# Moving gathers and low-part subtractions between GpSimd and VectorE in a three-layer interaction network

## The reference

```
prev = x
for k in 0, 1, 2:
    z = outer product of x and prev over the fields, for each example b and each of the 16 columns e
    t = z @ w[k] + bias[k]
    t = t / sqrt(sum of t*t over the units and the 16 columns)
    prev = t
features = concatenation of the three t, summed over e
```

## Time and profile before

| what | value |
|---|---|
| median of three runs | 1063.23 us (1059.57 to 1064.48) |
| the profiled execution's own time | 1061.89 us |
| its span, first to last instruction | 1060.2 us |
| PE busy | 1027.2 us, 97% |
| DVE busy | 974.6 us, 92% |
| POOL busy | 872.0 us, 82% |
| ACT busy | 795.4 us, 75% |

### The profile page before, as it was taken

One profiled execution on the slowest core, in us unless ns is written; L12 is line 12 of the kernel. 1 busy time (PEld: TensorE's weight loads), 2 busy tenths in 40 slices (PEclk: granted clock), 3 DMA queues, 4 the chain that ended last, 5 costly groups with the idle time before them and its releaser, 6 DMA issues.

```text
span 1060.2 us, 17970 instructions
## 1 busy us (share of the span) xinstructions
PE 1027.2 (97%) x4320; PEld 783.9 (74%) x4320; DVE 974.6 (92%) x3344; ACT 795.4 (75%) x2655; POOL 872.0 (82%) x729
## 2 busy tenths in 40 slices
PE   2899999999999999999999999999999999999998
PEld 1477777777777787777777777777777777788884
DVE  2699999999999999999999999999999999999993
ACT  3477877778687787878788787877878777888872
POOL 6788979889798988979798897989889798777770
PEclk9999999999999999999999999999999999999999
DMA  6550030302304030030303012030300303000000
GB/s 190 129 147 6 5 87 4 88 2 63 85 4 88 3 81 11 12 80 2 89 3 84 7 17 75 3 89 2 80 12 12 80 3 89 1 1 1 2 1 1
DMA packets 75893, 46.10 MB, mean 43 GB/s; under 512 B 55690, under 2 KB 58634, under 8 KB 75659
## 3 DMA queue, kind: packets, MB, share of 16 engines
q1 hardware_dynamic: 68487, 38.59, 15.1%
q0 software_dynamic: 5120, 1.29, 1.4%
q10 hardware_dynamic: 2179, 5.07, 1.4%
HBM read 42.99 MB, written 1.94 MB: 42 GB/s over the span
## 4 chain that ended last, share of the span: by engine, by line
PE 44%; POOL 39%; issue 7%; DVE 4%; DMA 2%; ACT 2%; SPq 1%; POOLq 0%; DVEq 0%; ACTq 0%
POOL sums L439 28%; POOL gathered L422 11%; PE bank_d L729 7%; PE bank_d L731 6%; PE bank_d L730 6%; PE bank_a L729 6%; PE bank_a L731 6%; PE bank_a L730 6%; PE acc L785 5%; DVE sums L953 2%; ACT scaled L567 1%; DMA x_pairs<-x_scratch 1%; PE bank_d L880 1%; PE turned L772 1%; PE bank_a L835 1%
## 5 line engine op out<-in xcount | busy, mean ns | idle before, releaser
L439 POOL TENSOR_TENSOR sums<-sums,scaled 128x512 f32<-128x512 f32 (+1 forms) x512 | 658.9, 1288 | 126.8 <-ACT scaled L567 88.9
L953 DVE SCALAR_TENSOR_TENSOR sums<-bank_d,x_col,sums 128x128 f32<-128x128 f32 x2304 | 654.6, 338 | 36.2 <-PE bank_d L731 17.6
L567 ACT ACTIVATE scaled<-bank_a,x_col 128x128 f32<-128x128 f32 x1920 | 555.4, 383 | 143.7 <-PE bank_a L731 135.7
L729 PE MATMUL bank_d<-w_hi,prev_lo 128*128 128x512 f32 x640 | 282.8, 442 | 6.2 <-DVE sums L972 2.2
L729 PE MATMUL bank_a<-w_hi,prev_lo 128*128 128x512 f32 (+1 forms) x640 | 268.5, 420 | 2.0 <-DVE prev_lo L1055 0.7
L731 PE MATMUL bank_d<-w_hi,prev_hi 128*128 128x512 f32 x640 | 252.5, 394 | 0.0
L730 PE MATMUL bank_d<-w_lo,prev_hi 128*128 128x512 f32 x640 | 252.2, 394 | 0.0
L731 PE MATMUL bank_a<-w_hi,prev_hi 128*128 128x512 f32 (+1 forms) x640 | 245.5, 384 | 0.0
L730 PE MATMUL bank_a<-w_lo,prev_hi 128*128 128x512 f32 (+1 forms) x640 | 244.8, 383 | 0.0
L567 ACT ACTIVATE sums<-bank_a,x_col 128x128 f32<-128x128 f32 x512 | 146.5, 370 | 68.6 <-PE bank_a L731 68.5
L422 POOL DMA_INDIRECT gathered<-in_table,idx x160 | 170.0, 1063 | 28.4 <-issue 18.1
(11 more groups left out here) (84 smaller groups left out, 541.9 us busy)
## 6 DMA issues: line engine op xcount, KB each, us to landing
x_pairs<-x_scratch SPq DMA_DIRECT2D x135, 156.0 KB
x_pairs<-x_scratch SPq DMA_DIRECT2D x96, 78.0 KB
gathered<-in_table,idx POOLq DMA_INDIRECT x160
x_sq<-x_scratch SPq DMA_DIRECT2D x32, 64.0 KB
x_pairs<-x_scratch SPq DMA_DIRECT2D x92, 22.0 KB
x_scratch<-gathered SPq DMA_DIRECT2D x16, 72.0 KB, 2.2
w_raw<-in_w ACTq DMA_DIRECT2D x1, 1024.0 KB, 4.9
w_raw<-in_w ACTq DMA_DIRECT2D x1, 896.0 KB, 10.0
```

Of the source, the lines that this page charges most:

```text
L439: nc.gpsimd.tensor_tensor(out=sums[:, n % SUMS, 0:w, :], in0=sums[:, n % SUMS, 0:w, :], in1=scaled[:, a - 1, 0:w, :], op=ALU.add).then_inc ...
L567: op = nc.scalar.activation(to[:, i, :], bank_a[at % A_RING][:, i * UNITS:(i + 1) * UNITS], ACT.Copy, scale=x_of(c, q, a * PER_BANK + i))
L729: nc.tensor.matmul(to, lo, w_h, start=True, stop=False)
L953: nc.vector.scalar_tensor_tensor(out=taken(n, u) if u in LEFT else total, in0=taken(n, u), scalar=x_of(c, q, A_FIELDS + u), in1=total, op0 ...
```

## The change

1. The ten gathers of chunk c, for c from 4 to 15, are spread over seven steps: one in step 6 and two in step 7 of round c - 3, then two in step 0, one in step 1, two in step 2, one in step 3 and one in step 4 of round c - 2. Chunk 3 keeps two in each of five steps. Chunk 2's last three stay in step 0 of round 0.
2. `low` moves from GpSimd to VectorE. A call at step n, place a, of GpSimd becomes one behind field `min(4 a + 7, 19)` of step n in VectorE's order.
3. SyncE issues the loads of the top weights before it waits for the gathers of chunk 5 and stores it, not behind that.
4. `CTX_STEP` goes from step 0 to step 6 of round 5.

```diff
+LOWS_AT = {item: (n, min(4 * a + 7, D_FIELDS - 1)) for item, (n, a) in HALVES_AT.items()}
...
+GATHERS_AT = {(0, 1 + j - GATHERS_BEFORE): (2, j) for j in range(GATHERS_BEFORE, GATHERS)}
+for _c in range(3, CHUNKS):
+    _places = [(step_at(_c - 2, _q), _a) for _q in range(5) for _a in (1, 2)]
+    if _c > 3:
+        _places = [(step_at(_c - 3, 6), 1), (step_at(_c - 3, 7), 1), (step_at(_c - 3, 7), 3)] + \
+            [(step_at(_c - 2, _q), _a) for _q, _a in ((0, 1), (0, 3), (1, 2), (2, 1), (2, 3), (3, 1), (4, 1))]
+    GATHERS_AT.update({at: (_c, j) for j, at in enumerate(_places)})
...
-CTX_STEP = step_at(5, 0)
+CTX_STEP = step_at(5, 6)
...
-            def low(k, c):
-                pool.wait_ge(prev_hi_made[k], c + 1)
-                nc.gpsimd.tensor_tensor(out=prev_lo[k][:, c % 2, :], in0=prev[:, k - 1, :],
-                                        in1=prev_hi[k][:, c % 2, :].bitcast(f32),
-                                        op=ALU.subtract).then_inc(prev_lo_made[k], 1)
-
...
                 for a in range(A_BANKS):
                     add_bank(A_BANKS * n + LEAD + a)
-                    if 1 <= a <= per_step and first + a - 1 < GATHERS:
-                        gather(it + 2, first + a - 1)
-                    for item, at in HALVES_AT.items():
-                        if at == (n, a):
-                            low(*item)
+                    if (n, a) in GATHERS_AT:
+                        c, j = GATHERS_AT[n, a]
+                        if j == 0:
+                            start_chunk(c)
+                        gather(c, j)
...
-                if c + 1 < CHUNKS:
-                    store_chunk(c + 1)
                 if c == 4:
...
                     sp.dma_start(top2_sb, w_top2.rearrange("(k p) n -> p k n", p=128)).then_inc(top_loaded, 16)
+                if c + 1 < CHUNKS:
+                    store_chunk(c + 1)
...
+            def low(k, c):
+                dve.wait_ge(prev_hi_made[k], c + 1)
+                nc.vector.tensor_tensor(out=prev_lo[k][:, c % 2, :], in0=prev[:, k - 1, :],
+                                        in1=prev_hi[k][:, c % 2, :].bitcast(f32),
+                                        op=ALU.subtract).then_inc(prev_lo_made[k], 1)
+
             for n in range(NJ):
                 for u in range(D_FIELDS):
...
+                    for item, at in LOWS_AT.items():
+                        if at == (n, u):
+                            low(*item)
```

## The result

Over 20 runs each, the changed kernel takes 1065.78 us (median; 1062.15 to 1069.84), the kernel before 1060.76 (1058.95 to 1064.48). The ratio is 1.0037, with a 95% interval of 1.0027 to 1.0047: slower by 0.4%, within the 0.5% that I called no change. The forecast was 1064.2, from a base of 1063.23, the median of three runs; the 20 runs put that base at 1060.76, so the change cost 5.0 us where the forecast had 1.0. The profiled execution took 1066.39 us by itself, with a span of 1064.6, 4.4 more than the span of before.

The account below looks back on a forecast made before the run. GpSimd's lateness, passed through VectorE to TensorE's ring, was taken as the bound. Steady rounds 0.0, top weights -1.9, start +1.2, rounds 14 and 15 +1.2, split +0.5: +1.0, so a median of 1064.2 us, range 1054 to 1073.

Parts of the forecast that it names:

- The chain GpSimd, VectorE, TensorE's ring: In a round: GpSimd late, VectorE waiting 1.4 us for it, TensorE held up 1.0 us at its ring of three banks.
- the predicted bound: Steps 4 and 5 of rounds 2 to 13: relieving GpSimd gains at most 0.93 us a round, 11.2 us in all.
- The low of step 1: Steady rounds: this subtraction, moved to VectorE, hardly waits for GpSimd and costs 0.65 us.
- The low of step 5: Steady rounds: this subtraction on VectorE waits on average half a GpSimd add, 0.55 us, and costs 1.15 us.
- L905: VectorE instruction in step 2, mean 1.69 us: set later against GpSimd's add, it loses about 0.2 us a round.
- Adding up VectorE's work: Steady round: VectorE's work of 61.4 us plus 0.7 waiting for TensorE gives 62.1, a change of 0.0.
- the lock is hit at its worst: Rival, chance 0.20, slower: step 5's low always begins with a GpSimd add, costs 1.9 us; +9.8 in all, 1074 us.
- TensorE's pace is reached: Rival, chance 0.33, faster: lows fall into GpSimd's gaps at 0.6 us each, giving 1057 us, or 1053 at full gain.
- The top weights: Round 3: loads issued before the wait for chunk 5's gathers remove its excess, -1.9 us; bounds -1.9 and 0.
- The start: From 60 to 112 us, VectorE has no wait to give up: two lows there cost +1.2 us.
- Rounds 14 and 15: Four lows on VectorE without relief by gathers, partly covered by TensorE's ring: +1.2 us; bounds 0 and 4 x 1.9.
- The split: Context split moved from step 0 to step 6 of round 5: +0.5 us; bounds -1.0 and +1.9.

Follow-up runs that it names:

- the kernel with field 11: The changed kernel with the low of step 5 behind field 11 of VectorE's order in place of field 7: 1053.28 us, ratio to before 0.9922.
- field 13: The changed kernel with the low of step 5 behind field 13 of VectorE's order in place of field 7, run once: 1059.17 us.
- the fastest version: The changed kernel with the lows back on GpSimd and the context split in step 7 of round 14 and step 3 of round 15: 1048.84 us.

## Why the prediction was right or wrong

The time is 0.15% from the forecast and inside the range, and the change lies within 0.5%, but that is luck: in the steady rounds two errors cancelled, and outside them the start (1.3 us too dear) and the end of the loop (1.2 too cheap) did.

- **The chain GpSimd, VectorE, TensorE's ring** was right. Both numbers came out: VectorE's waits for GpSimd went to none, and the gain of the gathers alone is the predicted bound, 0.93 a round. The gathers in steps 7 and 0, which I costed at nothing, lengthen step 7 by 0.4 us in rounds 1 and 9 of the kernel with the gathers alone, and in no steady round of the changed one.
- **The low of step 1** at 0.65: measured 0.70.
- **The low of step 5** is the term that failed: "it waits on average half an add", 1.15. It is 1.65 in every round from 2 to 14. An average over the phases is wrong where the phases repeat: all thirteen lows met the add at the same point, 0.2 behind its start. The exclusive lock that the Trainium skill states (page "SBUF — State Buffer", section "SBUF: two separate sides") agrees with the table above: lows of 0.68 to 1.65, by the rest of the add. My worst case for it, 1.9, was not reached; 1.65 is the most.
- **L905** at -0.2 a round: measured -0.9 (1.69 to 0.79 in the mean). In the steady rounds it is -1.2 (1.90 to 0.74). This is the error that cancelled the last one. Not by beginning later against the add, as I had it: it still begins within 0.02 us of one (546.28 and 546.26), but now the add is the one that takes longer.
- **Adding up VectorE's work** was the wrong kind of sum. I had 61.4 of work and 0.7 of waits; it is 60.64 and 1.2. The round is not set by VectorE's total but by one late bank in step 5. With a low of 0.68 there, step 5 is 7.00, 0.05 from TensorE's pace; beyond that each 0.1 of the low is 0.1 of the round. So the rival "the lock is hit at its worst" had the mechanism, and from its "mean of about 1.55" on it put the time at over 1069 (1064.2 and 5.2). It gave only back what the gathers had earned, because the base of my sum was too high by the same amount. The rival "TensorE's pace is reached" is the kernel with field 11: 1053.28, where I had 1053 to 1057.
- **The top weights** at -1.9: measured -1.8 in round 3, but not by this part. The gathers' plan alone brings round 3 to its neighbours' length; the part wins its 1.9 only beside the old gathers. I had noted that the gathers end sooner and gave that no price.
- **The start** at +1.2: -0.1 in rounds 0 and 1 (+0.6, -0.6); the lows there cost 0.70 and 1.16, and GpSimd's, at 1.3 and 2.0 before, no longer stood in VectorE's way. **Rounds 14 and 15** at +1.2: +2.4. The low of the last chunk behind field 19 alone takes 1.63 us; step 5 of round 15 grew from 7.06 to 8.58.
- **The split** at +0.5: +1.0. At step 6 it costs 2.0, and 0.42 where it and the product behind it miss GpSimd's adds; the part had no term for such a meeting. Its own reason (nothing left to earn back) is what step 0 shows.
- My sum didn't have the fall of the clock at the start. The profiled run of the kernel before had none, that of the changed one had it: 2.3 of the 4.4 us. The changed kernel's three executions without it took 1062.15 to 1063.47.

## What to carry to other kernels

Where two engines take turns at a shared resource and the loop repeats exactly, don't price a meeting at its average: find from the timeline where in the other's instruction the new one will begin, and try two or three places, since four VectorE fields of distance were worth 12.5 us here. Price the parts of a change one at a time as well as together; of two parts that relieve the same engine or the same wait, the second may have nothing left to win and only its cost to add. Work that is needed only at the end (here the split) belongs where the pipeline empties.

## What the runs showed of the hardware

- A VectorE subtraction of two SBUF tensors (128 x 512) takes 0.68 to 0.70 us alone, and 0.83, 1.11, 1.25 and 1.65 beside an add of GpSimd: always the rest of that add and some 0.55 more. When it gets in between two adds, the second is the one that stretches: the same two adds take 2.80 us there (field 11) and 2.46 where the low comes behind the start of the second (field 13).
- Where the two begin within 0.04 us of each other, either can be the one that takes longer: 1.90 for VectorE's L905 before (0.74 after), 1.92 for GpSimd's add after (1.28 by itself).
- The granted clock of TensorE fell to 0.64 (32 to 34 us) and 0.51 (34 to 36 us) in the changed kernel, which is the lower of its two levels, 1.2 GHz, for most of that time; TensorE was shown busy 1.73 of the 2.00 us before it, and 8.61 of the first 30. That does not tell the two cases apart: with the lows back on GpSimd it was busy 2.00 and 9.01 and the clock fell to 0.75 and 0.50, in the kernel before 2.00 and 8.26 and it stayed. From 36 us on it was back at 1.00, 2.4 GHz. In the fastest version the mean of 36 to 40 us was still 0.64, and the first transpose came at 70.4, against 68.8 in the changed kernel and 66.2 in the kernel with the new gathers alone, whose clock didn't fall.
